# First eight units' K/V and Q products one unit ahead, a new order in the quantising steps, probabilities scaled by GpSimd there

## The chip, the core and the metric

The kernel runs on one core of one Trainium2 chip. The metric is the device time of one launch in microseconds. A core has five engines that run side by side, each through its own queue of instructions in order: TensorE (PE in the rows, with its weight loads as PEld), VectorE (DVE), ScalarE (ACT), GpSimd (POOL) and SyncE (SP, which here only issues transfers). They meet at semaphores: an instruction waits until a counter has reached a value.

## What is computed

Two layers over x, 8 batches of 128 tokens of width 512. A layer is cross attention to a context of the same size (32 query heads and 8 key/value heads of 128, a root-mean-square norm on q and k), added through a tanh gate, and then a feed-forward part, also gated. The first layer's feed-forward multiplies quantised weights and inputs; the second's has 4-bit weights.

```
x = x + tanh(g_xattn[0]) * xattn0(layernorm(x), ctx)
x = x + tanh(g_ffn[0])   * mx_ffn(layernorm(x))
x = x + tanh(g_xattn[1]) * xattn1(layernorm(x), ctx)
x = x + tanh(g_ffn[1])   * int4_linear(layernorm(x))

q = rmsnorm(x @ Wq.T); k = rmsnorm(ctx @ Wk.T); v = ctx @ Wv.T
out = softmax(q k.T / sqrt(128) + mask) v;  return out @ Wo.T
mx_ffn: weights and inputs rounded in blocks of 32 with one power of two
        (weights to 4 bits, inputs to 6)
```

## The kernel before, in words

**Units.** The attention of both layers is cut into 128 units. A unit is one group (one key/value head and its four query heads, 8 groups a layer) for one batch; `n` counts them, and eight in a row share their weights. All products are done in three parts, high x high, low x high and high x low, of values split into a rounded part and the rest, so every operand has a `_hi` and a `_lo`. Rounding to `_hi` is a ScalarE copy, `_lo` a subtraction on VectorE or GpSimd.

**A unit's chain.** TensorE: K and V from the context into bank psKV, Q from the normalised tokens into psQ. ScalarE: squares of K and of the four heads of Q with their sums, V to `v_hi`. GpSimd: `unit_rstd`, the reciprocal root of the five sums (L519, L523). ScalarE scales K to `kn` (L709), VectorE scales Q to `qn` (L1020). TensorE transposes both; `kT` is taken out of the bank by VectorE (L1039), `qT` by ScalarE (L730). TensorE: scores into psSQ. VectorE: scale and mask to `probs` (L1007), then the negative maximum (L902). ScalarE: exponentials and row sums (L639). VectorE: `rinv` (L956), `probs` times `rinv` (L982). TensorE transposes them into psPO; ScalarE takes `pT_hi`, VectorE `pT_lo` (L907). TensorE multiplies with V; ScalarE takes `oT_hi`, VectorE `oT_lo` (L968). TensorE multiplies with the output weights into psY; VectorE adds that to x (L1049).

**Steps.** The chain is spread over four steps: step n does K/V and Q of unit n, the scores of n-1, the transposed probabilities and values of n-2 and the output of n-3. Each engine runs a function `step` of its own, called by `run_steps` for all n; the order of the statements in these functions is the order of the queue, and nothing else sets it. There are five kinds of steps: FIRST (n 0 to 7), QUANT (8 to 47, a loop over groups with eight steps in its body), ZONE (48 to 87, which holds the first feed-forward part), PLAIN (a loop) and LAST.

**FIRST.** It also loads the tokens and the context (two tiles of 128 tokens at a time), normalises a token tile (`moments` on VectorE, `ln_rstd_of` on GpSimd, `normalise`), has TensorE transpose it into psC and splits it (`xT_upper`, `xT_lower`); `t.first` names the tile that a step prepares, the one after its own. The first group's weights are split by `first_upper` and `first_lower` or `first_output_lower`.

**QUANT.** Beside its unit a step splits pieces of the next group's weights, ten a group, at the steps of `SPLIT_STEPS` (0, 1, 2, 1, 2, 1, 2, 1 pieces): `split_upper` on ScalarE (L652), `split_lower` on GpSimd (L485). And in seven of eight steps it quantises a piece of the feed-forward weights (512 columns in step 0, 384 in the others), with VectorE's `piece_scaled` (L830 to L846) and GpSimd's `round_piece` (L532, L534, L537); one step later VectorE turns it (`piece_turned`, L854) and ScalarE copies it away (L696). GpSimd's queue in a step is `split_lower`, `unit_rstd`, `round_piece`.

**ZONE.** Where a feed-forward tile is worked on (`t.active`), GpSimd scales the probabilities (L560) and ScalarE takes `kT`; elsewhere VectorE does both.

## Time and profile before

| | us |
|---|---|
| median of three timed runs | 1380.63 (1380.35 to 1380.7) |
| the profiled execution | 1378.14 |
| its span in the trace | 1376.3 |
| steps 0 to 7 (K/V product of unit 0 at 13.24, of unit 8 at 98.71) | 85.47 |
| steps 8 to 47 | 395.89 |
| step 48 | 10.04 |
| the rest | 871.66 |

Over the span TensorE is busy 98%, VectorE 72%, ScalarE 59%, GpSimd 48%. A share is a mean over stages. What a stage could gain is read from the time between two like instructions of TensorE in neighbouring steps, here the first of the K/V products, against the same time in a stage without waits.

### The profile page before, as it was taken

The numbers are of one execution on the slowest core, as the hardware profiler recorded it, in microseconds if no ns is written. First come the engines' busy times: TensorE is split into PE (matmuls) and PEld (weight loads), VectorE is DVE, ScalarE is ACT, GpSimd is POOL, SyncE is SP. The second block draws the span as 40 slices with busy tenths as digits, with TensorE's granted clock in tenths as the row PEclk, the third lists the DMA queues.
The fourth block names the chain that finished last, engine by engine and source line by source line (L and its number), as shares of the span: only waits on it lengthen the run. The fifth ranks groups of instructions, "written<-read, shape, count | busy, mean of one in ns | idle before, by whom it ended". The sixth has DMA issues, their size and how long they took to land.

```text
span 1376.3 us, 25625 instructions
## 1 busy us (share of the span) xinstructions
PE 1345.1 (98%) x7788; PEld 1130.0 (82%) x7804; DVE 988.4 (72%) x2016; ACT 814.6 (59%) x3255; POOL 660.0 (48%) x686
## 2 busy tenths in 40 slices
PE   4999999999999999999999999999999999999999
PEld 3888888888888888877777788888888888888887
DVE  4678888887888879678887866766555555655656
ACT  4656656565665666555566555655665666655542
POOL 2536656565665657446667533532333324242232
PEclk9999999999999999999999999999999999999999
DMA  8011021212112021010200011201010010100001
GB/s 284 1 47 55 20 64 47 65 48 65 48 32 81 17 66 53 10 36 12 77 32 1 1 31 47 77 31 55 32 46 30 0 47 30 46 30 1 1 9 54
DMA packets 33852, 59.47 MB, mean 43 GB/s; under 512 B 2800, under 2 KB 26224, under 8 KB 29680
## 3 DMA queue, kind: packets, MB, share of 16 engines
q1 hardware_dynamic: 33776, 58.54, 13.0%
q8 instruction: 38, 0.62, 0.2%
q14 instruction: 38, 0.31, 0.1%
HBM read 56.43 MB, written 2.10 MB: 43 GB/s over the span
## 4 chain that ended last, share of the span: by engine, by line
PE 68%; DVE 11%; issue 8%; ACT 7%; POOL 3%; DMA 1%; SPq 0%; ACTq 0%; DVEq 0%; POOLq 0%
PE bank L1164 46%; PE bank L1156 7%; PE bank L1249 5%; PE bank L1298 5%; ACT probs L639 3%; PE bank L1190 3%; DVE pT_lo L907 2%; DVE probs L1007 2%; DVE negmax L902 1%; PE bank L1306 1%; DVE fw_y L838 1%; DVE amax L830 1%; ACT w_hi L652 1%; ACT oT_hi L660 1%; ACT qT L730 1%
## 5 line engine op out<-in xcount | busy, mean ns | idle before, releaser
L485 POOL TENSOR_TENSOR w_lo<-w_raw,w_hi (+1 forms) x150 | 226.8, 1528 | 251.0 <-ACT w_hi L652 251.0
L679 ACT ACTIVATE squares<-bank 128x128 bf16<-128x128 f32 x512 | 134.7, 278 | 217.9 <-PE bank L1164 217.9
L639 ACT ACTIVATE probs<-probs,negmax 128x128 f32<-128x128 f32 x512 | 198.7, 391 | 73.3 <-DVE negmax L902 71.0
L1007 DVE SCALAR_TENSOR_TENSOR probs<-bank,mask_sb 128x512 f32<-128x512 f32 x127 | 87.5, 689 | 204.4 <-PE bank L1249 204.4
L523 POOL TENSOR_TENSOR rstd<-meansq,scalars 128x5 f32<-128x5 f32 x128 | 156.3, 1221 | 10.9 <-POOL meansq L519 1.3
L519 POOL TENSOR_TENSOR meansq<-sumsq,scalars 128x5 f32<-128x5 f32 x128 | 27.4, 214 | 273.6 <-ACT squares L679 273.6
L1164 PE MATMUL bank<-w_hi,oT_hi 128*128 (+1 forms) x512 | 150.9, 416 | 0.0
L1164 PE MATMUL bank<-w_hi,xT_hi 128*128 (+1 forms) x512 | 140.3, 395 | 0.6 <-DVE w_lo L804 0.6
L1164 PE MATMUL bank<-w_lo,oT_hi 128*128 (+1 forms) x512 | 138.2, 391 | 0.0
L1164 PE MATMUL bank<-w_hi,xT_lo 128*128 (+1 forms) x512 | 137.5, 390 | 0.0
L1164 PE MATMUL bank<-w_hi,oT_lo 128*128 (+1 forms) x512 | 137.5, 390 | 0.0
L1164 PE MATMUL bank<-w_lo,xT_hi 128*128 (+1 forms) x512 | 137.2, 390 | 0.0
L1249 PE MATMUL bank<-kT,qT 128*128 128x128 f32 x1024 | 135.2, 275 | 0.0
L1249 PEld LDWEIGHTS bank<-kT,qT 128*128 128x128 f32 x1024 | 124.5, 192 | 0.1
L709 ACT ACTIVATE kn<-bank,rstd 128x128 f32<-128x128 f32 x128 | 47.1, 368 | 115.2 <-POOL rstd L523 115.1
L968 DVE TENSOR_TENSOR oT_lo<-bank,oT_hi 128x512 fp32r<-128x512 f32 x125 | 85.6, 685 | 41.2 <-ACT oT_hi L660 40.4
L1164 PEld LDWEIGHTS bank<-w_lo,oT_hi 128*128 128x128 f32 x512 | 96.2, 188 | 22.5
L1164 PEld LDWEIGHTS bank<-w_lo,xT_hi 128*128 128x128 f32 x512 | 96.1, 188 | 21.4
L1164 PEld LDWEIGHTS bank<-w_hi,oT_lo 128*128 128x128 f32 x512 | 96.1, 188 | 20.6
L1164 PEld LDWEIGHTS bank<-w_hi,xT_lo 128*128 128x128 f32 x512 | 96.1, 188 | 20.0
L679 ACT ACTIVATION_READ_ACCUMULATOR squares<-bank 128x1 f32 x512 | 106.2, 207 | 0.0
L1164 PEld LDWEIGHTS bank<-w_hi,xT_hi 128*128 128x128 f32 x512 | 88.2, 190 | 12.6 <-DVE w_lo L804 0.9
(143 smaller groups left out, 3076.4 us busy)
## 6 DMA issues: line engine op xcount, KB each, us to landing
w_raw<-in_wq SPq DMA_DIRECT2D x16, 1024.0 KB, 4.9
w_raw<-in_wo SPq DMA_DIRECT2D x16, 1024.0 KB, 4.7
fw_raw<-in_ffn_w SPq DMA_DIRECT2D x36, 192.0 KB, 2.3
w_raw<-in_wk SPq DMA_DIRECT2D x16, 256.0 KB, 5.4
w_raw<-in_wv SPq DMA_DIRECT2D x16, 256.0 KB, 5.4
x_sb<-in_x SPq DMA_DIRECT2D x4, 512.0 KB, 9.9
ctx_raw<-in_ctxT SPq DMA_DIRECT2D x4, 512.0 KB, 10.5
fw_raw<-in_ffn_w SPq DMA_DIRECT2D x7, 256.0 KB, 2.6
```

What stands on the lines that cost most here:

```text
L485: last = nc.gpsimd.tensor_tensor(lo, raw, hi.bitcast(FP32), ALU.subtract)
L523: nc.gpsimd.tensor_tensor(rstd[:, :], meansq[:, :], minus_half[:, :], ALU.pow).then_inc(rs_done, 1)
L639: last = nc.scalar.activation(probs[:, h * P:(h + 1) * P], probs[:, h * P:(h + 1) * P], ACT.Exp, bias=negmax[:, h:h + 1], accum_out=rowsum ...
L679: last = nc.scalar.activation(squares[:, h // 2, (b + 1) % 4, h % 2, :], psQ[:, h * P:(h + 1) * P], ACT.Square, scale=SCALE, accum_out=sum ...
L709: nc.scalar.activation(kn[:, :], psKV[:, 0:P], ACT.Copy, scale=rstd[:, REP:REP + 1]).then_inc(kn_done, 1)
L968: nc.vector.tensor_tensor(oT_lo[:, :], psPO[:, :], oT_hi[:, :].bitcast(FP32), ALU.subtract).then_inc(o_lod, 1)
L1007: nc.vector.scalar_tensor_tensor(heads(probs[:, :]), heads(psSQ[:, :]), SCALE, mask_sb[:, :].unsqueeze(1).to_broadcast([P, REP, P]), ALU.m ...
L1156: last = nc.tensor.transpose(dst[:, k * P:(k + 1) * P], src[:, k * P:(k + 1) * P], m)
L1164: last = nc.tensor.matmul(dst, left(a, k), right(b, k), start=(n == 0), stop=(n == len(terms) - 1))
L1190: last = nc.tensor.matmul(ps[:, 0:width], f_xqT[:, k, :], wT[:, col:col + width], start=(k == 0), stop=(k == KT - 1))
L1249: last = nc.tensor.matmul(psSQ[:, h * P:(h + 1) * P], qT[:, h * P:(h + 1) * P], kT[:, :], start=True, stop=True)
L1298: last = nc.tensor.matmul(psPO[:, :], v[:, slot, :], p[:, :], start=(k == 0), stop=(k == 2))
```

## The change

**In FIRST.** Tokens and context are loaded tile by tile, the first of each on ScalarE's queue, in another order (and the context lies in memory by batch). TensorE does K/V and Q of unit n+1 in step n (`first_kv`, `first_q`), with psA and psB as second banks for odd units; Q of unit 7 stands at the end of step 6, and step 7 has neither. Unit 0's Q is done part by part as the pieces are rounded and subtracted. Tile n+2 is prepared in step n. Splits of group 1 come one step later, the first output weights' subtractions go from GpSimd to VectorE, and 37 transposes of the identity into psSQ (`keep_clock`), whose results nobody reads, stand ahead of the first K/V product.

**In QUANT.** TensorE does the scores ahead of the transposed probabilities. ScalarE does the exponentials of a unit at the head of the next step instead of before `kT` and `qT`, the roundings of the weight pieces between V and the squares of Q, and `kT`. VectorE takes the piece's maximum and then `rinv` behind `oT_lo`, and `pT_lo` ahead of `qn`. GpSimd scales the probabilities first, then does the root, then the rounding, and `split_lower` last. Step 48 takes over the exponentials that step 47 leaves. SyncE's `load_group` waits for `kv_ps` too.

Three places show what the queues hold. First, **GpSimd** in a step of QUANT with two split pieces, before:

```order
L485 TENSOR_TENSOR w_lo<-w_raw,w_hi 128x512
...
L485 TENSOR_TENSOR w_lo<-w_raw,w_hi 128x512
...
L519 TENSOR_TENSOR meansq<-sumsq,scalars 128x5
L523 TENSOR_TENSOR rstd<-meansq,scalars 128x5
...
L532 TENSOR_TENSOR fw_y<-fw_y,fw_magic 128x384
L534 TENSOR_TENSOR fw_y<-fw_y,fw_magic 128x384
L537 TENSOR_TENSOR fw_out<-fw_y,blk_pow 128x384
```

and in the change (`w_lo` is a weight piece, `rstd` the unit's roots, `fw_` the quantised piece):

```order
L560 TENSOR_TENSOR probs<-probs,rinv 128x512
...
L519 TENSOR_TENSOR meansq<-sumsq,scalars 128x5
L523 TENSOR_TENSOR rstd<-meansq,scalars 128x5
...
L532 TENSOR_TENSOR fw_y<-fw_y,fw_magic 128x384
L534 TENSOR_TENSOR fw_y<-fw_y,fw_magic 128x384
L537 TENSOR_TENSOR fw_out<-fw_y,blk_pow 128x384
...
L494 TENSOR_TENSOR w_lo<-w_raw,w_hi 128x512
...
L494 TENSOR_TENSOR w_lo<-w_raw,w_hi 128x512
```

The root moved ahead of the two pieces, and the scaling of the probabilities is new at the head.

Second, **VectorE** in such a step, before:

```order
L854 STREAM_TRANSPOSE fw_turned<-fw_out 128x384
L968 TENSOR_TENSOR oT_lo<-bank,oT_hi 128x512
L982 TENSOR_TENSOR probs<-probs,rinv 128x512
...
L987 TENSOR_TENSOR v_lo<-bank,v_hi 128x128
...
L830 TENSOR_REDUCE amax<-fw_raw 128x12
...
L1007 SCALAR_TENSOR_TENSOR probs<-bank,mask_sb 128x512
L1020 TENSOR_TENSOR qn<-bank,rstd 128x512
L907 TENSOR_TENSOR pT_lo<-bank,pT_hi 128x512
L902 TENSOR_REDUCE negmax<-probs 128x4
L1039 TENSOR_SCALAR kT<-bank,scalars 128x128
L1049 SCALAR_TENSOR_TENSOR x_sb<-bank,scalars,x_sb 128x512
```

and in the change:

```order
L877 STREAM_TRANSPOSE fw_turned<-fw_out 128x384
L1003 TENSOR_TENSOR oT_lo<-bank,oT_hi 128x512
...
L843 TENSOR_REDUCE amax<-fw_raw 128x12
L925 RECIPROCAL rinv<-rowsum 128x4
...
L1022 TENSOR_TENSOR v_lo<-bank,v_hi 128x128
...
L1046 SCALAR_TENSOR_TENSOR probs<-bank,mask_sb 128x512
L934 TENSOR_TENSOR pT_lo<-bank,pT_hi 128x512
L942 TENSOR_TENSOR qn<-bank,rstd 128x512
L929 TENSOR_REDUCE negmax<-probs 128x4
L1082 SCALAR_TENSOR_TENSOR x_sb<-bank,scalars,x_sb 128x512
```

`rinv` moved behind the maximum of the piece, `pT_lo` ahead of `qn`, and the scaling and `kT` are gone.

Third, **TensorE** at the start, from unit 0's query product to the transposes of its K and Q, before (bank0 and bank1 are psKV and psQ):

```order
L1164 MATMUL bank1<-w_hi,xT_hi 128x512 x4
L1164 MATMUL bank1<-w_lo,xT_hi 128x512 x4
L1164 MATMUL bank1<-w_hi,xT_lo 128x512 x4
L1156 MATMUL bank7<-ident,f_s 128x128 x4
L1289 MATMUL bank0<-ident,kn 128x128
L1156 MATMUL bank2<-ident,qn 128x128 x4
```

and in the change, from the last third of that product on:

```order
L1210 MATMUL bank1<-w_hi,xT_lo 128x512 x4
L1210 MATMUL bank5<-w_hi,ctx_hi 128x256 x4
L1210 MATMUL bank5<-w_lo,ctx_hi 128x256 x4
L1210 MATMUL bank5<-w_hi,ctx_lo 128x256 x4
L1210 MATMUL bank6<-w_hi,xT_hi 128x512 x4
L1210 MATMUL bank6<-w_lo,xT_hi 128x512 x4
L1210 MATMUL bank6<-w_hi,xT_lo 128x512 x4
L1202 MATMUL bank7<-ident,f_s 128x128 x4
L1291 MATMUL bank0<-ident,kn 128x128
L1202 MATMUL bank2<-ident,qn 128x128 x4
```

Unit 1's K/V and Q, in bank5 and bank6, moved in front of unit 0's transposes.

The diff, cut to its core:

```diff
 SPLIT_STEPS = {1: (0,), 2: (1, 2), 3: (3,), 4: (4, 5), 5: (6,), 6: (7, 8), 7: (9,)}
-SPLIT_STEPS_FIRST = {2: (0, 1), 3: (2, 3), 4: (4, 5), 5: (6, 7), 6: (8, 9)}
+SPLIT_STEPS_FIRST = {3: (0, 1), 4: (2, 3), 5: (4, 5), 6: (6, 7), 7: (8, 9)}
...
-        self.first = s + 1 if kind == FIRST and s + 1 < BATCHES else None
+        self.first = s + 2 if kind == FIRST and s + 2 < BATCHES else None
...
+        def exp_after(kind):
+            return kind == QUANT
...
+        def kv_bank(n, kind):
+            return psA if kind == FIRST and n % 2 else psKV
+        def q_bank(n, kind):
+            return psB if kind == FIRST and n % 2 else psQ
...
+                sp.wait_ge(kv_ps, freed)
                 sp.wait_ge(q_ps, freed)
...
+            load_kv(0, 0, loaded_kv0)
+            sp.dma_start(x_sb[:, 1, :], x[P:2 * P, :]).then_inc(loaded_x[1], 16)
+            load_q(0, 0, loaded_q0)
+            sp.dma_start(ctx_raw[:, 1, :], ctxT[:, 1, :]).then_inc(loaded_ctx[1], 16)
+            sp.dma_start(norm_sb[:, :], norms).then_inc(loaded_small, 16)
+            sp.dma_start(mask_sb[:, :], mask).then_inc(loaded_small, 16)
+            load_tokens(2)
+            load_tokens(3)
+            load_wo(0, 0, loaded_wo0)
+            load_tokens(4)
             sp.dma_start(gates[:, 0:2], g_xattn.partition_broadcast(P)).then_inc(loaded_gates, 16)
             sp.dma_start(gates[:, 2:4], g_ffn.partition_broadcast(P)).then_inc(loaded_gates, 16)
-            load_x(0)
-            load_kv(0, 0, loaded_kv0)
-            load_ctx(0)
-            sp.dma_start(norm_sb[:, :], norms).then_inc(loaded_small, 16)
-            sp.dma_start(mask_sb[:, :], mask).then_inc(loaded_small, 16)
-            load_q(0, 0, loaded_q0)
-            load_x(1)
-            load_ctx(1)
-            load_wo(0, 0, loaded_wo0)
-            for t in (2, 3):
-                load_x(t)
-                load_ctx(t)
+            load_tokens(5)
+            load_tokens(6)
+            load_tokens(7)
             load_q(1, WSLOT, loaded_qkv)
             load_kv(1, WSLOT, loaded_qkv)
             load_wo(1, WSLOT, loaded_wo)
...
+                if t.active or kind == QUANT:
                     pool.wait_ge(rinv_done, n - 1)
                     nc.gpsimd.tensor_tensor(
...
+                if kind in (ZONE, PLAIN):
+                    split_lower(split_pieces(n, b, kind, j))
                 if t.first is not None:
                     ln_rstd_of(t.first)
-                if t.last is not None:
-                    ln_rstd_of(NORM["last", t.last])
-                split_lower(split_pieces(n, b, kind, j))
                 if has(n, 0):
                     unit_rstd(n)
+                if kind == FIRST:
+                    split_lower(split_pieces(n, b, kind, j))
...
                     round_piece(q, b)
+                if kind == QUANT:
+                    split_lower(split_pieces(n, b, kind, j))
...
-            act.wait_ge(loaded_gates, 32)
-            nc.scalar.activation(tanh_gates[:, :], gates[:, :], ACT.Tanh).then_inc(gates_done, 1)
+            act.dma_start(x_sb[:, 0, :], x[0:P, :]).then_inc(loaded_x[0], 16)
+            act.dma_start(ctx_raw[:, 0, :], ctxT[:, 0, :]).then_inc(loaded_ctx[0], 16)
...
+                exp_late = exp_after(kind) or (kind == FIRST and b == BATCHES - 1)
...
-                split_upper(split_pieces(n, b, kind, j))
+                if exp_after(kind) or (kind == ZONE and n == ZONE0):
+                    softmax_exp(n - 1)
+                if kind in (ZONE, PLAIN):
+                    split_upper(split_pieces(n, b, kind, j))
...
+                if kind == QUANT:
+                    split_upper(split_pieces(n, b, kind, j))
...
+                if t.first is not None:
+                    ctx_upper(t.first)
+                if kind == FIRST and b in (1, 2):
+                    if b == 1:
+                        act.wait_ge(loaded_wo0, 16)
+                    first_upper(WO_PIECES[2 * b - 2:2 * b])
+                if kind == FIRST:
+                    scaled_k(n, kind)
...
+                if kind == FIRST:
+                    split_upper(split_pieces(n, b, kind, j))
+                if t.first is not None:
+                    xT_upper(t.first)
...
+                if has(n, 0) and kind != FIRST:
+                    scaled_k(n, kind)
+                if has(n, 1) and t.next is None and t.down is None and not exp_late:
                     softmax_exp(n)
...
+                    if t.active or kind == QUANT:
...
+                if kind == FIRST and b == 0:
+                    act.wait_ge(loaded_gates, 32)
+                    nc.scalar.activation(tanh_gates[:, :], gates[:, :], ACT.Tanh).then_inc(gates_done, 1)
...
+            ctx_upper(0)
             act.wait_ge(loaded_kv0, 32)
-            for k in KV_PIECES:
-                raw, hi, _ = weight_piece(0, k)
-                nc.scalar.activation(hi, raw, ACT.Copy).then_inc(first_hi, 1)
-            ctx_upper(0)
+            first_upper(KV_PIECES)
             xT_upper(0)
             act.wait_ge(loaded_q0, 16)
             first_upper(Q_PIECES)
+            ctx_upper(1)
+            xT_upper(1)
...
-                    dve.wait_ge(exp_done, n - 1)
-                    nc.vector.reciprocal(rinv[:, :], rowsum[:, :]).then_inc(rinv_done, 1)
+                    if kind != QUANT:
+                        row_inverse(n)
...
-                if has(n, 2) and not t.active:
+                if q is not None and b < QSTEPS:
+                    piece_maximum(q, b)
+                if kind == QUANT:
+                    row_inverse(n)
+                if has(n, 2) and not t.active and kind != QUANT:
                     dve.wait_ge(rinv_done, n - 1)
                     nc.vector.tensor_tensor(heads(probs[:, :]), heads(probs[:, :]), each(rinv[:, :], P),
                                             ALU.mult).then_inc(pn_done, 1)
...
+                    if t.first is not None:
+                        ctx_lower(t.first)
...
+                if kind == FIRST:
+                    scaled_q(n, kind, t)
...
-                if has(n, 2) and t.gate is not None:
+                if has(n, 2) and (t.gate is not None or kind == QUANT):
                     probs_lower(n)
...
+                if has(n, 0) and kind != FIRST:
+                    scaled_q(n, kind, t)
+                if has(n, 2) and qn_first(kind, t) and kind != QUANT:
                     probs_lower(n)
                 if has(n, 1) and qn_first(kind, t):
                     maximum(n)
...
+                if has(n, 0) and not t.active and kind != QUANT:
...
+                if t.first is not None:
+                    xT_lower(t.first)
...
+                if kind == FIRST and b + 3 < BATCHES:
+                    dve.wait_ge(loaded_x[b + 3], 16)
+                    moments(b + 3, b + 3)
+                if kind == FIRST and b in (1, 2):
+                    for k in WO_PIECES[2 * b - 2:2 * b]:
+                        first_lower(k, k + 1)
+                if kind == FIRST and b == 1:
+                    dve.wait_ge(gates_done, 1)
+                    nc.vector.tensor_scalar(down_gate[:, :], tanh_gates[:, LAYERS:LAYERS + 1], 1 / FP6_UNIT, None,
+                                            ALU.mult).then_inc(down_gate_done, 1)
...
+            ctx_lower(0)
             for n, k in enumerate(KV_PIECES):
                 first_lower(k, n + 1)
-            ctx_lower(0)
...
+            dve.wait_ge(loaded_x[1], 16)
+            moments(1, 1)
+            dve.wait_ge(xT_ps, 1)
+            normalise(1, 1, f_s[:, :])
             for n, k in enumerate(Q_PIECES):
                 first_lower(k, len(KV_PIECES) + n + 1)
+            ctx_lower(1)
...
+            xT_lower(1)
+            dve.wait_ge(loaded_x[2], 16)
+            moments(2, 2)
             dve.wait_ge(qkw_done, 1)
...
+            def first_kv(u):
...
+                pe.wait_ge(ctx_lo_done, u + 1)
+                if u == 0:
+                    pe.wait_ge(first_lo, len(KV_PIECES))
+                wait(pe, kT_sb, u - 1)
+                three_products(kv_bank(u, FIRST)[:, 0:2 * P], lambda a, k: (ctx_hi, ctx_lo)[a][:, u, k * P:(k + 1) * P],
+                               lambda a, k: (w_hi, w_lo)[a][:, WKV0 + k * 2 * P:WKV0 + (k + 1) * 2 * P]).then_inc(kv_ps, 1)
+            def first_q(u, part=slice(0, 3 * KT)):
+                pe.wait_ge(xT_lod, u + 1)
+                wait(pe, qn_done, u - 1)
+                return three_products(q_bank(u, FIRST)[:, :], lambda a, k: (xT_hi, xT_lo)[a][:, k, xT_tile(u)],
+                                      lambda a, k: (w_hi, w_lo)[a][:, WQ0 + k * REP * P:WQ0 + (k + 1) * REP * P], part)
...
+                if kind == FIRST and b == BATCHES - 2:
+                    first_kv(b + 1)
+                    scores()
+                    probabilities()
+                    output()
+                    transposed()
+                    values()
+                    first_q(b + 1).then_inc(q_ps, 1)
+                    return
+                if kind == FIRST and b == BATCHES - 1:
+                    scores()
+                    probabilities()
+                    output()
+                    transposed()
+                    values()
+                    return
+                if kind == FIRST and b + 1 < BATCHES:
+                    first_kv(b + 1)
+                    first_q(b + 1).then_inc(q_ps, 1)
...
+                if kind == QUANT:
+                    scores()
                 if has(n, 2):
...
+                    probabilities()
+                if has(n, 1) and kind != QUANT:
+                    scores()
...
+            def keep_clock(count):
...
+                for _ in range(count):
+                    nc.tensor.transpose(psSQ[:, 0:P], ident[:, :], ident[:, :])
             pe.wait_ge(consts, 2)
+            keep_clock(21)
             pe.wait_ge(ln_xn, 1)
             transposes(f_s, psC, ident[:, :]).then_inc(xT_ps, 1)
+            keep_clock(16)
+            first_kv(0)
+            for k in range(KT):
+                pe.wait_ge(first_hi, len(KV_PIECES) + k + 1)
+                first_q(0, slice(k, k + 1))
+            pe.wait_ge(ln_xn, 2)
+            pe.wait_ge(xT_lod, 1)
+            transposes(f_s, psC, ident[:, :]).then_inc(xT_ps, 1)
+            for k in range(KT):
+                pe.wait_ge(first_lo, len(KV_PIECES) + k + 1)
+                first_q(0, slice(KT + k, KT + k + 1))
+            first_q(0, slice(2 * KT, 3 * KT)).then_inc(q_ps, 1)
             run_steps(pe, step)
```

## Rows read from the trace of the kernel before

**Rows 1.** Stretches: from:to, length, busy us of each engine, clock, DMA share, GB/s

```profile
98.71:494.60 395.89, 390.56 (x2242) 329.12 (x2241) 330.48 (x716) 241.10 (x1000) 243.29 (x235) 1.00 0.17 52
494.60:504.64 10.04, 9.93 (x58) 8.27 (x56) 8.25 (x20) 6.51 (x30) 4.21 (x5) 1.00 0.15 41
504.64:1376.30 871.66, 866.36 (x5071) 726.93 (x5085) 587.35 (x1173) 509.64 (x2023) 374.42 (x391) 1.00 0.10 31
196.99:207.36 10.37, 10.00 (x58) 8.10 (x57) 9.02 (x20) 6.35 (x26) 7.70 (x8) 1.00 0.16 36
982.94:992.47 9.53, 9.53 (x58) 8.30 (x56) 5.30 (x12) 5.79 (x25) 3.13 (x3) 1.00 0.28 107
```

**Rows 2.** Timeline of a long quantising step: start, length, engine, line, operation

```profile
160.65 2.99 POOL L485 TENSOR_TENSOR w_lo<-w_raw,w_hi  x2 [2.40 <-ACT w_hi L652]
...
162.47 1.20 DVE L835 TENSOR_SCALAR inv_pow<-amax 128x12 uint32<-128x12 uint32 x1
...
163.87 1.56 POOL L523 TENSOR_TENSOR rstd<-meansq,scalars 128x5 f32<-128x5 f32 x1
...
165.31 0.68 DVE L1007 SCALAR_TENSOR_TENSOR probs<-bank,mask_sb 128x512 f32<-128x512 f32 x1
...
165.91 0.68 DVE L1020 TENSOR_TENSOR qn<-bank,rstd 128x512 f32<-128x512 f32 x1
```

**Rows 3.** Waits in 98.7 to 494.6: total us, times, longest

```profile
PEld bank L1156 <- DVE qn L1020: 9.2, 15, 0.6
PEld bank L1164 <- DVE kT L1039: 6.3, 20, 0.3
```

**Rows 4.** Timeline of the first 45 us

```profile
0.74 0.40 SPq L414 DMA_DIRECT2D scalars<-in_g_xattn  x1
...
1.66 0.43 SPq L386 DMA_DIRECT2D x_sb<-in_x  x1
...
7.54 0.69 DVE L786 BATCH_NORM_STATS2 ln_stats<-x_sb 128x6 f32<-128x512 f32 x1 [7.54 <-DMA x_sb<-in_x]
...
11.96 1.23 DVE L809 TENSOR_TENSOR ctx_lo<-ctx_raw,ctx_hi 128x1024 fp32r<-128x1024 f32 x1 [0.70 <-ACT ctx_hi L618]
...
13.56 2.19 ACT L613 ACTIVATE w_hi<-w_raw 128x512 fp32r<-128x512 f32 x4 [1.15 <-DMA w_raw<-in_wq]
...
19.87 0.28 ACT L679 ACTIVATE squares<-bank 128x128 bf16<-128x128 f32 x1 [3.13 <-PE bank L1164]
...
34.50 1.19 PE L1164 MATMUL bank<-w_hi,ctx_hi 128*128 128x256 f32 x4
```

**Rows 5.** Stretches of the first stage, two steps

```profile
34.50:46.65 12.15, 9.91 (x48) 8.72 (x49) 6.76 (x12) 8.42 (x31) 7.64 (x8) 0.78 0.01 2
79.16:89.20 10.04, 10.04 (x62) 8.79 (x62) 8.13 (x15) 6.81 (x27) 5.08 (x6) 1.00 0.01 3
```

**Rows 6.** Timeline of TensorE in a quantising step with one split piece

```profile
168.09 0.75 PE L1164 MATMUL bank<-w_hi,ctx_hi 128*128 x4
...
172.38 0.60 PE L1156 MATMUL bank<-ident,probs 128*128 128x128 f32 x4
172.82 1.06 PE L1249 MATMUL bank<-kT,qT 128*128 128x128 f32 x8
173.63 1.18 PE L1164 MATMUL bank<-w_hi,oT_hi 128*128 x4
...
176.59 0.60 PE L1156 MATMUL bank<-ident,qn 128*128 128x128 f32 x4
176.95 0.48 PE L1298 MATMUL bank<-pT_hi,v_hi 128*128 128x512 f32 x1
```

**Rows 7.** Groups by shape: busy us, mean ns; quantising stage, then GpSimd's scaling in the zone

```profile
L485 POOL TENSOR_TENSOR w_lo<-w_raw,w_hi x39 | 61.8, 1597 | 64.5 <-ACT w_hi L652 64.5
L639 ACT ACTIVATE probs<-probs,negmax 128x128 f32<-128x128 f32 x120 | 46.8, 391 | 52.5 <-DVE negmax L902 52.5
```

```profile
L560 POOL TENSOR_TENSOR probs<-probs,rinv 128x512 f32<-128x512 f32 x15 | 15.6, 1042 | 25.6 <-DVE rinv L956 25.6
```

201 lines of the change are left out of this document (87 added, 114 removed).

## The prediction

> **What bounds the kernel now.** I cut the trace at the starts of TensorE's K/V products, one stretch per step of the schedule, then read one long step of the quantising stage in order of time, the waits of that stage, and the start. TensorE is busy for 390.56 of 395.89 us in one stage and for 866.36 of 871.66 in the rest [rows 1]. So what another engine does costs time only where TensorE waits or runs at its lower clock, and the reader should look for the steps that are longer than TensorE's own work. A step of the second layer, where nothing is waited for, takes 9.53 us [rows 1]; that is what the matmuls and transposes of one unit need. Against this floor two stages are long.
>
> The **quantising stage** (units 8 to 47) takes 395.89 us, 9.90 a step; 40 x 9.53 would be 381.2, so 14.7 us are lost there. They sit mostly in three steps of each eight, which take 10.37 instead of 9.64 [rows 1]: those in which two weight pieces are split. In one of them, in order of time [rows 2], GpSimd subtracts two pieces (2.99 us, to 163.64), and only then makes the unit's reciprocal root (163.87 to 165.43); VectorE's tiny `inv_pow` takes 1.20 while GpSimd works, though it has 12 columns; VectorE's `probs` and `qn` follow, the last done at 166.59, and TensorE waits for `qn` [rows 3]. The other 0.1 of each short step is the wait for `kT` before the next K/V product [rows 3].
>
> The **first stage** (units 0 to 7) lasts until 98.71. Unit 0's query product ends at 19.8 (ScalarE's squares of it start at 19.87, [rows 4]), and from there each unit's chain from its query product to its own transposes lies bare. The step from 34.50 has TensorE busy 9.91 of 12.15 us at a granted clock of 0.78; the last but one takes 10.04 at 1.00 [rows 5].
>
> **First stage, part by part.** *Loads.* The first token tile is half the size and is issued first, on ScalarE's queue, while SyncE starts on the K/V weights. Before, two tiles were issued at 1.66, 0.9 us behind the first small issue, and landed at 7.54 [rows 4]; without the 0.9 and with half the bytes (0.26 MB, shared with the K/V weights, some 0.4) I take 6.2. The query weights landed at 13.56 [rows 4] with 1.6 MB ahead of them; with 1.3 MB ahead and the stream 0.9 us earlier they land at 11.8. *Unit 0.* ScalarE rounds the four query pieces in 2.19 [rows 4], to 14.0. VectorE, which has normalised the second tile meanwhile, subtracts four times (0.68 each, as `qn` in [rows 2]), to 16.9. The last four products end at 17.9: 1.9 us earlier than now. *Units 1 to 7.* From there TensorE has K/V and Q of the next unit to do while the squares, root, scaled K and scaled Q of this one are made. Its work, from one step's rows [rows 6]: K/V and Q 4.2; transposed probabilities 0.44; scores 0.81; output product and transposed K 2.96; transposed Q 0.36; values 0.78. With the next tile's transposes (10.04 less 9.53, so 0.5) step 0 needs 5.2, step 1 6.0, step 2 7.2, steps 3 to 5 10.0 each, step 6 9.5, and step 7, which has no K/V and Q any more, 5.3. Sum 63.2, so 81.1 if nothing waits.
>
> What waits next is **VectorE** in steps 1 and 2. A full step of it is 8.13 busy [rows 5]. In step 2 it has no output residue and no accumulation (two passes, 1.4), but a context residue (half of the 1.23 of two tiles, [rows 4]) and two output weight pieces that GpSimd did before (1.3): 8.6 against TensorE's 7.2. Step 1 has three passes fewer again, 7.1 against 6.0. That is 2.5 us; with 0.4 for unit 0's root, which is done a little after TensorE comes to it, the stage ends at **84.0**, 14.7 us earlier. The filler transposes run while TensorE has nothing else and cost nothing themselves; what they are worth is the clock. Bounds: 81.1 with no wait, and 89, if three K/V products run at the lower clock as that of 34.50 did (its first four matmuls took 1.19, [rows 4], so twelve some 2.7, against 1.5 at the higher) with 1.3 us more in the loads.
>
> **Quantising stage, part by part.** I write a step from the start of its K/V product. *TensorE*: scores now stand at 4.3 and the transposed probabilities at 5.1, output at 5.5, transposed Q at 8.5, values at 8.9, next step 9.6 [rows 6]; without waits 0.1 less each. *ScalarE*: the output copy to 0.8, then the exponentials (four of 0.39, [rows 7]) to 2.5, K's square and V to 3.0, two roundings to 4.2, just before the query product is there at 4.4. So moving the roundings costs nothing, and moving the exponentials takes `rinv` from 1.3 to 2.6. *GpSimd* scales the probabilities from 2.7 in 1.04 (its own time for this in the zone, [rows 7]) to 3.8. TensorE needs them at 5.0: 1.2 to spare. It starts the root at 5.8, to 7.0 alone and to 7.4 at its 1.56 [rows 2]; rounds for 2.9 (its 7.70 of a long step less splits and root, [rows 1, 2]), to 10.2; then subtracts up to two pieces at 1.6 each [rows 7], to 13.4, which is 3.8 of the next step. *VectorE* loses two passes (probabilities and `kT`). Its piece takes 2.84 from `inv_pow` to `probs` [rows 2], with the tiny operation ahead 3.1, and 2.1 without the blocked 1.0; started at 3.4 and let in at 3.8, it gives `probs` 5.9 to 6.6, the residue to 7.2, `qn` at 7.4 to 8.1. TensorE comes to it at 8.4. `kT`, now ScalarE's first work behind its transpose, is ready 0.4 before it is needed, which takes the 0.1 of the short steps away.
>
> What is late next is the steps **behind two split pieces** (steps 3 and 5 of eight) and the one behind the 512-wide piece (step 1): GpSimd starts the scaling at 3.8 only, holds to 4.9, and VectorE's tiny operations, blocked as `inv_pow` was [rows 2], come through at 4.9. Then `probs` ends at 7.5, the residue at 8.1, `qn` at 8.8: TensorE waits 0.4. Three such steps in each of five groups are 6.0, so the stage takes 381.2 + 6.0 = **387.2**, 8.7 less. Bounds: 381.2 (no wait) and 395.2, if all 35 steps that have a piece wait 0.4.
>
> A rule speaks against the GpSimd part. The rows show 1.04 on GpSimd for a pass of the size that takes VectorE 0.68, a ratio of 1.5 [rows 2, 7]. The Trainium skill, GPSIMD Engine Reference, section 4.1 Engine selection, says to use VectorE for elementwise work on a tile, GpSimd being about 2 times slower with two inputs. By that page's ratio the scaling would take an estimated 1.4, end at 5.2 behind two pieces, after TensorE's 5.0, and cost an estimated 3 us more. I go by the row.
>
> **Zone.** From 504.64 on the order is the same, and its 871.66 us stay [rows 1]. Unit 48's step has ScalarE do one more unit of exponentials before its squares, so `rinv` comes at 2.6 and VectorE's scaling, which stands behind its output residue and the piece's maximum there, at 4.9 instead of in time; with its piece behind that, `pT_lo` comes some 1.4 late. The step takes 11.0 instead of 10.04 [rows 1]: +1.0 (bounds 0 and 2). The one more wait in SyncE's weight loads is met together with the old one; behind it stand only loads that are needed a group later.
>
> **Sum**, against the profiled execution: 1378.14 - 14.7 - 8.7 + 1.0 = 1355.7. The three timed runs have a median of 1380.63, 2.5 above the profiled one; I forecast on their level, **1358.2**.
>
> **Rivals.**
> *All waits gone.* First stage to 81.1, quantising 381.2, unit 48 +0.5: 17.6 + 14.7 - 0.5 = 31.8 less, 1348.8. For it: by the steps above each engine but TensorE has time to spare in nearly every step. Against: the blocked 1.20 [rows 2].
> *The two engines block each other in every step.* Scaling and piece start close together in all of them, so the 0.4 comes 35 times: quantising 395.2, and with the rest as forecast 1366.2. By the row one blocked operation costs 1.0; whether all of them are blocked, it doesn't tell. The Trainium skill, SBUF — State Buffer, section Who interferes with whom, says that GpSimd and a VectorE instruction with two inputs in SBUF lock each other out for a whole instruction. It would favour this case, and the 1.20 [rows 2] agrees with it as far as one operation can.
> *The start gains little.* TensorE is at most half busy between 12.5 and 17, and the step from 34.50, behind such a pause, began at half clock. Three cold K/V products (1.2 each) and loads 1 us later: stage to 88.6, 1362.8.
> *Slower.* Each piece of VectorE meets the scaling (1.04) and the root as well, so that `qn` comes at 8.1 + 1.0 + 1.3 = 10.4 and 35 steps wait 2.0: quantising 451, sum 1422. It is slower than before from a mean step of 10.24 on (the 13.7 us of the other parts spread over 40 steps of 9.90). Against: GpSimd has 7.70 + 1.04 = 8.7 us of work in the fullest step [rows 1, 7], under 9.53, and the order puts the root ahead of the long subtractions.
>
> **How the numbers follow.** Forecast 0.50, all waits gone 0.20, blocking in every step 0.16, weak start 0.09, slower 0.05. The range reaches from the second case to a little above the third and fourth, 1349 to 1370; about 2 in 10 are left out, the slow case and the tails. A measurement of this kernel can tell about 0.2%, 2.8 us, from no change. Faster by more than that 0.93, within it 0.02, slower 0.05.
>
> **What would show it.** First stage: the K/V product of unit 8 at 84 instead of 98.71, the first squares at 18, and a granted clock of 1.00 from unit 1 on. Quantising: steps of 9.53 to 9.55 after one split piece, 9.9 after two; the waits for `kT` gone, that for `qn` left at some 6 us; `inv_pow` still far over 0.2 in the mean. A scaling that ends after 5.0 of its step, or a TensorE that waits for `probs`, would make the forecast wrong; so would a first K/V product later than 12.

## The result and the profile after

The changed kernel takes 1346.98 us (median of 4 runs, 1346.24 to 1347.88), the kernel before beside it 1380.49 (4 runs). The ratio is 0.9762 (95% interval 0.9745 to 0.9779): 33.5 us faster. The forecast was 1358.2, with a range down to 1349. The direction held, and the gain was half as large again as foretold. What came true, within 2 us, is the rival in which all waits go (1348.8).

The profiled execution took 1346.36 us, its span is 1344.4. Cut into the same stretches as before [rows 1] (from:to, length, busy us of PE, PEld, DVE, ACT, POOL, granted clock, DMA share, GB/s):

```profile
0.00:81.13 81.13, 77.63 (x459) 66.09 (x460) 58.66 (x119) 55.27 (x201) 33.80 (x52) 1.00 0.39 139
81.13:462.57 381.44, 381.44 (x2241) 333.65 (x2242) 299.32 (x636) 265.78 (x1045) 263.97 (x276) 1.00 0.17 53
462.57:472.81 10.24, 10.16 (x57) 8.19 (x56) 7.71 (x19) 6.65 (x32) 4.41 (x5) 1.00 0.16 44
472.81:1344.40 871.59, 867.33 (x5087) 726.96 (x5085) 587.39 (x1173) 509.22 (x2023) 373.93 (x391) 1.00 0.09 31
128.90:138.43 9.53, 9.53 (x57) 8.34 (x56) 7.98 (x17) 6.55 (x27) 7.70 (x9) 1.00 0.09 24
```

Unit 8's K/V product starts at 81.13 (98.71 before, 84.0 forecast). The quantising stage takes 381.44 (395.89 before, 387.2 forecast), and TensorE is busy in all of it. Step 48 takes 10.24 (10.04; 11.0), the rest 871.59 (871.66). The last row is a step behind one with two split pieces, the kind for which 9.9 was forecast: it takes 9.53, as all but the first do (9.64). The profile's page follows the chain of work that ended last. TensorE has 96% of that chain now, and had 68% before:

```profile
PE 96%; DVE 1%; POOL 1%; issue 1%; DMA 0%; ACT 0%; SPq 0%; POOLq 0%; DVEq 0%; ACTq 0%
```

The start, in order of time (start, length, engine, line, operation); it answers to [rows 4]:

```profile
0.73 0.39 ACTq L610 DMA_DIRECT2D x_sb<-in_x  x1
...
3.59 0.69 DVE L804 BATCH_NORM_STATS2 ln_stats<-x_sb 128x6 f32<-128x512 f32 x1 [3.59 <-DMA x_sb<-in_x]
...
6.49 1.16 ACT L617 ACTIVATE w_hi<-w_raw 128x512 fp32r<-128x512 f32 x2 [0.66 <-DMA w_raw<-in_wv]
...
8.60 0.71 PE L1210 MATMUL bank<-w_hi,ctx_hi 128*128 128x256 f32 x4
...
9.66 2.19 ACT L617 ACTIVATE w_hi<-w_raw 128x512 fp32r<-128x512 f32 x4 [1.53 <-DMA w_raw<-in_wq]
...
15.36 0.28 ACT L694 ACTIVATE squares<-bank 128x128 bf16<-128x128 f32 x1 [1.46 <-PE bank L1210]
```

The token tile is used at 3.59 instead of 7.54 (forecast 6.2), the query weights are there at 9.66 instead of 13.56 (forecast 11.8), and the first squares start at 15.36 instead of 19.87.

The quantising step at 128.90, behind two split pieces; it answers to [rows 2]:

```profile
129.36 2.55 POOL L494 TENSOR_TENSOR w_lo<-w_raw,w_hi  x2
...
131.86 1.05 POOL L560 TENSOR_TENSOR probs<-probs,rinv 128x512 f32<-128x512 f32 x1
131.89 1.04 DVE L855 TENSOR_SCALAR amax<-amax 128x12 f32<-128x12 f32 x1
132.97 0.17 DVE L858 TENSOR_SCALAR inv_pow<-amax 128x12 uint32<-128x12 uint32 x1
...
133.98 0.60 PE L1202 MATMUL bank<-ident,probs 128*128 128x128 f32 x4
...
135.00 1.17 POOL L523 TENSOR_TENSOR rstd<-meansq,scalars 128x5 f32<-128x5 f32 x1
...
136.21 0.69 DVE L942 TENSOR_TENSOR qn<-bank,rstd 128x512 f32<-128x512 f32 x1
...
137.30 0.60 PE L1202 MATMUL bank<-ident,qn 128*128 128x128 f32 x4
```

Two things stand here. VectorE's first tiny operation beside the scaling takes 1.04 us, about as long as GpSimd scales, as forecast. But the two pieces take 2.55, not 3.2: GpSimd is free at 131.86, 2.96 after the step's start and not 3.8. So `qn` is done at 136.90, 8.0 after the start, 0.4 before TensorE comes to it. In the list of waits of this stage no wait of TensorE for another engine is left; the ones of [rows 3] are gone, both.

### The profile page after: what moved, and what is told of

It is laid out like the page before. It is cut to its first block, busy times and chain, and to the rows that moved or that the text cites. A ratio compares the mean times of both kernels' runs of the same rounds, so it can differ in the third digit from the quotient of the medians.

```text
span 1344.4 us, 25718 instructions
## 1 busy us (share of the span) xinstructions
PE 1336.6 (99%) x7841; PEld 1134.9 (84%) x7841; DVE 953.1 (71%) x1944; ACT 836.9 (62%) x3299; POOL 676.1 (50%) x722
## 4 chain that ended last, share of the span: by engine, by line
PE 96%; DVE 1%; POOL 1%; issue 1%; DMA 0%; ACT 0%; SPq 0%; POOLq 0%; DVEq 0%; ACTq 0%
PE bank L1210 66%; PE bank L1202 9%; PE bank L1274 8%; PE bank L1301 7%; PE bank L1236 3%; PE bank L1395 1%; PE bank L1291 1%; PE bank L1407 1%; DMA w_raw<-in_wv 0%; DVE w_lo L823 0%; PE bank L1382 0%; POOL probs L560 0%; POOL rstd L523 0%; DVE probs L1046 0%; POOL f_s L513 0%
## 5 line engine op out<-in xcount | busy, mean ns | idle before, releaser
L494 POOL TENSOR_TENSOR w_lo<-w_raw,w_hi (+1 forms) x150 | 210.7, 1420 | 174.9 <-ACT w_hi L661 174.9
L523 POOL TENSOR_TENSOR rstd<-meansq,scalars 128x5 f32<-128x5 f32 x128 | 153.6, 1200 | 10.7 <-POOL meansq L519 1.1
L1274 PEld LDWEIGHTS bank<-kT,qT 128*128 128x128 f32 x1024 | 127.5, 191 | 3.3
```

The costliest lines, as they stand in the source:

```text
L494: last = nc.gpsimd.tensor_tensor(lo, raw, hi.bitcast(FP32), ALU.subtract)
L523: nc.gpsimd.tensor_tensor(rstd[:, :], meansq[:, :], minus_half[:, :], ALU.pow).then_inc(rs_done, 1)
L1274: last = nc.tensor.matmul(psSQ[:, h * P:(h + 1) * P], qT[:, h * P:(h + 1) * P], kT[:, :], start=True, stop=True)
```

## The experiments

All are measured beside the kernel before. "After" means 1346.98 us with a quantising stage of 381.44. Times are medians of 4 runs (5 for order_to_55); starts and lengths of steps come from one trace each. Unit 0's part of the start varies from trace to trace: in the ten traces with the same loads, filler and order up to unit 0's query product, its K/V product starts between 8.52 and 9.82, and the query weights are used between 9.44 and 10.91. After has 8.60 and 9.66.

### The two halves apart

**start_only**: the new first stage, the old order in the quantising steps.

```
         def exp_after(kind):
-            return kind == QUANT
+            return False
...
-                if kind in (ZONE, PLAIN):
+                if kind in (QUANT, ZONE, PLAIN):
                     split_lower(split_pieces(n, b, kind, j))
...
-                if has(n, 2) and not t.active and kind != QUANT:
+                if has(n, 2) and not t.active:
```

> The first stage of the changed kernel with the quantising steps of the kernel before (VectorE scales the probabilities, the split pieces stand ahead of the root, the exponentials at their old place, kT on VectorE, scores after the transposes of the probabilities). Theory (the two halves are independent and add): unit 8's K/V product at 81.1 as in the changed kernel, units 8 to 47 take 395.9 as before, step 48 10.04, and the time is 1380.5 - 17.6 = 1362.9 us. Rival (the order in the quantising steps helps the start as well, or an early start leaves the first quantising step late): unit 8 later than 82, time over 1364.5.

1361.46 us. Unit 8 at 81.06, units 8 to 47 in 396.13.

**order_only**: the kernel before with the new quantising steps.

```
-                if t.active:
+                if t.active or kind == QUANT:
                     pool.wait_ge(rinv_done, n - 1)
...
                     round_piece(q, b)
+                if kind == QUANT:
+                    split_lower(split_pieces(n, b, kind, j))
...
+                if kind == QUANT or (kind == ZONE and n == ZONE0):
+                    softmax_exp(n - 1)
```

> The kernel before with the quantising steps of the changed one, and the first stage as before (its last exponentials move to step 8, as the new order needs). Theory (the halves add): unit 8 at 98.7, units 8 to 47 in 381.4, step 48 about 10.2, time 1380.5 - 14.3 = 1366.2 us; a split piece on GpSimd takes 1.3 us here instead of the 1.6 before, since it no longer lies beside VectorE's quantiser. Rival (the steps are short only after the new start): over 1370.

1366.18 us. Unit 8 came at 101.39, and from there to unit 48 it took 381.33. Against the runs of before beside them (1380.18) the halves give 18.7 and 14.0 us, 32.7 together, where both at once give 33.5: they add, within 1 us. In both the mean of a split piece came out as the order has it, 1.60 us with the old and 1.30 with the new.

That unit 8 came 2.7 us later than in the profile of before, in code that is the same up to there but for one group of exponentials, I put down to the clock. Most of it lies in unit 0's query product. Its first four matmuls, before and then in order_only, with the same start within 0.1 us:

```profile
16.78 1.21 PE L1164 MATMUL bank<-w_hi,xT_hi 128*128 128x512 f32 x4 [0.61 <-DVE w_lo L804]
```

```profile
16.84 2.08 PE L1183 MATMUL bank<-w_hi,xT_hi 128*128 128x512 f32 x4 [0.62 <-DVE w_lo L812]
```

The operands are there at the same time in both and TensorE waits for none within it; the clock is given as 1.00 for both, so that the durations alone speak for it here. The stretches of the first stage in order_only show a lower one in that column too:

```profile
13.29:26.19 12.90, 9.55 (x33) 7.62 (x34) 6.36 (x15) 4.72 (x17) 2.12 (x4) 0.93 1.06 389
26.19:37.34 11.15, 9.08 (x42) 7.61 (x42) 6.62 (x10) 6.55 (x24) 4.65 (x6) 0.78 0.49 169
37.34:49.05 11.71, 9.79 (x48) 8.13 (x49) 6.76 (x12) 7.92 (x31) 7.64 (x8) 0.82 0.01 2
49.05:60.30 11.25, 11.25 (x62) 9.73 (x61) 8.14 (x15) 7.41 (x27) 5.10 (x6) 0.88 0.00 1
```

With the old start TensorE pauses for 1.9 to 3.4 us in each of the first three steps, and the granted clock is under 1.00 in four. In the profiled run of before the clock was back at 0.96 in the fourth:

```profile
46.65:57.90 11.25, 11.21 (x63) 9.24 (x62) 8.38 (x15) 7.35 (x28) 5.08 (x6) 0.96 0.00 1
```

In the changed kernel that column gives 1.00 throughout the stage. Nearly all runs of before lie within 0.3 us of 1378.0 or of 1380.4, and few between; a start that in one run loses 1.9 us more in one product would make such levels. It isn't shown that it does: the mean clocks of the runs don't tell the levels apart (1377.99 and 1380.3 both have 0.998).

### What in the quantising steps carries the gain

**vector_scales**: VectorE scales the probabilities in them, as before; all else is changed.

```
-                if t.active or kind == QUANT:
+                if t.active:
                     pool.wait_ge(rinv_done, n - 1)
...
-                if has(n, 2) and not t.active and kind != QUANT:
+                if has(n, 2) and not t.active:
                     dve.wait_ge(rinv_done, n - 1)
```

> The changed kernel, but VectorE scales the probabilities in the quantising steps, in the place where GpSimd's scaling blocked it. Theory A (the GpSimd scaling gives VectorE little, because VectorE's next instruction took 0.73 us on average instead of 0.17 while GpSimd scaled): VectorE's chain ends 0.3 us later, the product's slack of 0.4 us before the transposes of qn takes it, and the time stays at 1346.5 to 1348.5 us. Theory B (GpSimd's scaling carries a good part of the 14.4 us that the quantising steps gained): 1352 us or more, with TensorE waiting for qn in every long step.

1347.56 us, the stage 381.43:

```profile
81.49:462.92 381.43, 381.43 (x2240) 333.61 (x2241) 306.38 (x676) 265.74 (x1045) 223.03 (x236) 1.00 0.17 53
```

The scaling on GpSimd is worth nothing that can be measured. VectorE is busy 306.38 us instead of 299.32, 7 more, although 40 passes went back to it: in the changed kernel it pays most of them as blocked time.

**splits_before_root**: GpSimd splits ahead of the root again, but behind the scaling.

```
-                if kind in (ZONE, PLAIN):
+                if kind in (QUANT, ZONE, PLAIN):
                     split_lower(split_pieces(n, b, kind, j))
...
-                if kind == QUANT:
-                    split_lower(split_pieces(n, b, kind, j))
```

> The changed kernel, but GpSimd splits the weight pieces ahead of the unit's root in the quantising steps, behind the scaling. Theory (where the splits stand is what the steps hang on): in a step with two pieces scaling ends at 4.0, two pieces beside VectorE's quantiser at 1.6 each end at 7.2, root at 8.8, qn at 9.5 and its transposes 1.1 us later than the TensorE work allows, x 15 such steps = 16.5 us: 1363.5 us; steps with one piece stay at 9.53; a piece takes 1.6 us on average. Rival (only the amount of GpSimd work counts): 1347 to 1349 and pieces of 1.3 us.

1369.01 us, 22.0 more than after. A step with two pieces takes 10.65 (10.6 by the theory). Of the four with a single piece in each eight, three take 9.71, 9.71 and 10.18 and not 9.53; the last one, in which nothing is quantised, stays at 9.53:

```profile
132.26:141.98 9.72, 9.72 (x57) 8.29 (x56) 8.65 (x18) 6.56 (x27) 6.45 (x8) 1.00 0.09 24
141.98:152.63 10.65, 9.95 (x57) 8.29 (x56) 9.55 (x18) 7.07 (x28) 8.11 (x9) 1.00 0.08 25
```

That the place of the pieces decides held, but the 10.6 came true by luck. The theory went over the root: two pieces of 1.6, then the root, then `qn`. In the step from 141.98 the root is over at 7.98, 0.8 earlier than laid out, and `qn` starts only at 8.73. What is late is VectorE, held up beside each piece:

```profile
145.60 2.52 POOL L494 TENSOR_TENSOR w_lo<-w_raw,w_hi  x2
145.70 1.20 DVE L856 TENSOR_SCALAR inv_pow<-amax 128x12 uint32<-128x12 uint32 x1
...
147.01 1.52 DVE L859 SCALAR_TENSOR_TENSOR fw_y<-fw_raw,inv_pow 128x384 f32<-128x384 f32 x1
...
148.67 1.29 POOL L523 TENSOR_TENSOR rstd<-meansq,scalars 128x5 f32<-128x5 f32 x1
...
150.71 0.68 DVE L940 TENSOR_TENSOR qn<-bank,rstd 128x512 f32<-128x512 f32 x1
```

`inv_pow` takes 0.17 and `fw_y` 0.56 where GpSimd is idle; here the two lose 2.0 us. The root alone would have let `qn` end at 8.7, for which TensorE would have waited some 0.3 (an estimate from these rows). In [rows 2] it was the same: the root was over at 165.43, and `qn` began at 165.91, behind VectorE's own chain.

A piece took 1.28, not 1.6, though the pieces now lay beside VectorE's quantiser, which I had taken for the cause. This is the quantising stage's group of pieces in start_only, and then in splits_before_root (count, busy us, mean ns):

```profile
L494 POOL TENSOR_TENSOR w_lo<-w_raw,w_hi (+1 forms) x51 | 80.8, 1596 | 83.9 <-ACT w_hi L659 83.9
```

```profile
L494 POOL TENSOR_TENSOR w_lo<-w_raw,w_hi (+1 forms) x51 | 64.7, 1281 | 0.0
```

What differs is seen in the timeline of start_only. A single piece takes 1.75 there, two take 2.99, so the second costs 1.24 and only the first is long:

```profile
133.80 1.75 POOL L494 TENSOR_TENSOR w_lo<-w_raw,w_hi  x1 [2.67 <-ACT w_hi L659]
...
143.21 0.68 DVE L1008 TENSOR_TENSOR probs<-probs,rinv 128x512 f32<-128x512 f32 x1
143.28 2.99 POOL L494 TENSOR_TENSOR w_lo<-w_raw,w_hi  x2 [2.40 <-ACT w_hi L659]
```

The first piece starts 0.07 into VectorE's scaling, a pass with two inputs in SBUF, and takes 0.45 longer than a piece alone. The "1.6 each" of [rows 7] is 1.28 a piece and one wait of 0.45 behind that pass: in each eight steps seven of the ten pieces are first ones, and 0.7 x 0.45 and 1.28 make 1.60. In splits_last_only, which follows, VectorE still scales and the pieces are moved: their mean is 1.30.

**splits_last_only**: start_only, and of the new order nothing but GpSimd's split pieces at the step's end.

```
-                if kind in (QUANT, ZONE, PLAIN):
+                if kind in (ZONE, PLAIN):
                     split_lower(split_pieces(n, b, kind, j))
...
                     round_piece(q, b)
+                if kind == QUANT:
+                    split_lower(split_pieces(n, b, kind, j))
```

> The new first stage with the old quantising steps, and of the new order only that GpSimd splits the weight pieces at the end of a step (after round_piece) instead of ahead of the root. Theory (the place of the split pieces is what the 14.4 us of the quantising steps hang on): the 10.34 us steps with two pieces become 9.63 like the others, 15 x 0.7 = 10.5 us, and steps 8 to 47 take 385 to 386: 1361.5 - 10.5 = 1351 us; what is left to 1347 are the waits of 0.1 us a step for kT. Rival (the move works only together with the early exponentials and scores, because a piece at the head of the next step blocks VectorE's scaling there): over 1356.

1348.59 us. The stage takes 383.79 instead of 396.13: moving these few lines gives 12.3 of its 14.7 us. VectorE's tiny operations take 0.17 each in it. What is left, 2.4 us, goes with the wait of TensorE's weight loads for `kT`, in 25 steps (they run ahead of the matmuls, so a wait of 0.3 makes a step only some 0.1 longer):

```profile
PEld bank L1204 <- DVE kT L1064: 6.4, 25, 0.3
```

**kT_on_vector**: after, with `kT` scaled by VectorE.

```
-                    if t.active or kind == QUANT:
+                    if t.active:
                         layer = layer_of(n, 0, kind)
                         act.wait_ge(kt_ps, n + 1)
...
-                if has(n, 0) and not t.active and kind != QUANT:
+                if has(n, 0) and not t.active:
                     dve.wait_ge(kt_ps, n + 1)
```

> The changed kernel, but VectorE scales kT again in the quantising steps. Theory (with pT_lo now ahead of qn only the maxima stand between qn and kT, which ends 0.5 us before the next unit's K/V product needs the bank): no step longer than 9.54, time 1346.5 to 1347.5 us. Rival (the move to ScalarE is what took the waits for kT away): 0.1 us again in each of 40 steps, 1351 us.

1346.95 us, no step of the stage over 9.54. So ScalarE's taking `kT` isn't needed either; together with splits_last_only it says that the last 2.4 us come from the rest of the new order. In it `pT_lo` stands ahead of `qn`, so that only the maxima are between `qn` and `kT`. Which of its parts is enough was not tried.

**scaling_twice**: after, with GpSimd scaling twice in each quantising step. The probabilities are divided by the row sums twice, so the values differ; the operations and their sizes are otherwise the same.

```
                     pool.wait_ge(rinv_done, n - 1)
+                    if kind == QUANT:
+                        nc.gpsimd.tensor_tensor(
+                            probs[:, :].rearrange("p (h c) -> p h c", h=REP), probs[:, :].rearrange("p (h c) -> p h c", h=REP),
+                            rinv[:, :].unsqueeze(2).to_broadcast([P, REP, P]), ALU.mult).then_inc(copied, 1)
+                        pool.wait_ge(copied, n - (BATCHES - 1))
```

> The changed kernel with GpSimd scaling the probabilities twice in each quantising step (so they are divided by the row sums twice, and the output isn't the reference's): 1.04 us more of the same work in the same place. It measures the slack behind the scaling. Theory: VectorE's chain (piece, masked scores, pT_lo, qn) moves back by the 1.0 us that its next instruction is blocked once more; the slack of 0.4 us before the transposes of qn takes part, 0.6 us stay in about 35 steps: 1347 + 20 = 1367 us, with waits for qn. Rival (there is slack all through the step, as the short steps suggest): 1347 to 1349 us.

1353.63 us, 6.7 more where 20 were expected, and the stage takes 388.16. Of each eight steps three stay at 9.53, the three behind two split pieces take 9.75, the one behind the 512-wide piece 9.78, and the one that has this piece itself 10.00. TensorE's waits in the stage (total, times, longest):

```profile
PEld bank L1208 <- DVE qn L948: 4.1, 10, 0.6
PEld bank L1208 <- POOL probs L566: 3.4, 15, 0.5
```

So the slack behind the scaling is 1.0 us or more in 15 steps, 0.8 in 20 and 0.6 in 5. The kinds of wait differ. Behind two pieces TensorE waits for the probabilities, the second scaling being over 5.2 after the step's start; the 10 waits for `qn` are in the other two kinds. The step from 111.80 (behind two pieces):

```profile
114.79 0.16 DVE L861 TENSOR_SCALAR amax<-amax 128x12 f32<-128x12 f32 x1
...
115.95 1.04 POOL L566 TENSOR_TENSOR probs<-probs,rinv 128x512 f32<-128x512 f32 x1
...
116.01 1.40 DVE L867 SCALAR_TENSOR_TENSOR fw_y<-fw_raw,inv_pow 128x384 f32<-128x384 f32 x1
...
117.04 0.42 PEld L1208 LDWEIGHTS bank<-ident,probs 128*128 128x128 f32 x4 [0.20 <-POOL probs L566]
```

I had expected VectorE's whole chain to slip by 1.04. Its first tiny operation slipped in ahead of the scaling (0.16), and the second scaling held `fw_y` up by 0.84, so the masked scores start 0.7 later than in the step shown of after. `qn` starts at 7.79 against 7.31, only 0.5 later: the other 0.2 are the time for which it had to wait for the root in after (over at 136.17).

### The first stage

**no_unit_ahead**: the products of units 1 to 7 at the head of their own step.

```
-                if kind == FIRST and b == BATCHES - 2:
+                if kind == FIRST and b:
+                    first_kv(b)
+                    first_q(b).then_inc(q_ps, 1)
+                if False:
...
-                if kind == FIRST and b == BATCHES - 1:
+                if False:
...
-                if kind == FIRST and b + 1 < BATCHES:
+                if False:
```

> The changed kernel, but in units 1 to 7 the K/V and Q products stand at the head of their own step again, in the order of before; loads, filler transposes and the tile preparation are as changed. Theory (being one unit ahead carries most of the first stage's gain beyond the 4.5 us at the very start): TensorE waits again for the chain squares, root, qn in each step, unit 8 at about 93, time 1359 us. Rival (the earlier loads, the full clock and the tile by tile preparation carry it): unit 8 before 84, time under 1350.

1363.95 us, unit 8 at 98.75: all 17.6 us gone. But TensorE waits here for something that this edit alone brings in, the next normalised tile:

```profile
PEld bank L1202 <- DVE f_s L810: 9.4, 5, 2.2
```

`f_s` stands behind the context's residue on VectorE, that behind ScalarE's rounding, and that behind the squares of this unit's query product, which is harmless only as long as the product came a step earlier.

**no_unit_ahead_ctx_early**: the same, with ScalarE rounding the context ahead of the squares.

```
                     nc.scalar.activation(v_hi[:, b % 4, :], kv_bank(n, kind)[:, P:2 * P], ACT.Copy).then_inc(v_hid, 1)
+                if t.first is not None:
+                    ctx_upper(t.first)
...
                     last.then_inc(sq_done, 1)
-                if t.first is not None:
-                    ctx_upper(t.first)
```

> As no_unit_ahead (products of units 1 to 7 at the head of their own step), with one thing mended: ScalarE rounds the next tile's context ahead of the unit's squares instead of behind them, so that VectorE's normalised tile no longer hangs on this unit's query product. Theory (being one unit ahead itself is worth most of the first stage, since in units 0 to 2 TensorE has nothing to do while squares, root and scaled query are made, some 3 us each, and falls to its lower clock there): unit 8's K/V product at 91 to 95, time 1357 to 1360 us. Rival (most of the 17 us that no_unit_ahead lost was the wait for the normalised tile, 8.5 to 9.4 us in its list): unit 8 before 90, time under 1356 us.

1359.21 us, unit 8 at 91.48, and the whole quantising stage at 9.53 a step. So being one unit ahead is worth 10.3 us of the 17.6, clock included. In the first three steps (11.86, 9.48 and 10.73) TensorE stands idle for 3.4, 2.5 and 2.1 us, and the granted clock is 0.90 to 0.94 up to the fourth; of the first:

```profile
9.02:20.88 11.86, 8.49 (x37) 5.47 (x38) 8.94 (x20) 6.25 (x20) 3.40 (x6) 0.90 0.94 341
```

There TensorE has too little else to do while squares, root and scaled query are made. Steps one unit ahead can't be laid beside these one by one, since theirs hold the next unit's products. From unit 4 on the steps take 9.97, as they do one unit ahead.

**gates_first**: the two small broadcast loads at the head of SyncE's queue.

```
+            sp.dma_start(gates[:, 0:2], g_xattn.partition_broadcast(P)).then_inc(loaded_gates, 16)
+            sp.dma_start(gates[:, 2:4], g_ffn.partition_broadcast(P)).then_inc(loaded_gates, 16)
             load_kv(0, 0, loaded_kv0)
```

> The changed kernel with the two small broadcast loads of the gates at the head of SyncE's queue, as before; x0 and ctx0 stay on ScalarE's queue, nobody waits for the gates before step 0. Theory (the broadcast loads were what made all data start late before, where the transfers moved nothing until 4.2 us): the K/V weights land 2 us or more later than at 6.5 us, unit 0's K/V product starts at 10.5 or later, and the time is 1349 us. Rival (they cost their two issues of 0.45 us and no more): product at 9.5, 1347.9 us.

1348.45 us. Their issues take 0.9 us, but unit 0's K/V product starts at 10.58, 2.0 us later than in after and 0.8 later than in the latest of the ten traces with the same start; the query weights are used at 11.63, unit 8 starts at 83.12. Even the tile on the other queue came later, at 4.67 where the other traces with it on that queue have 3.26 to 3.66:

```profile
4.67 0.69 DVE L804 BATCH_NORM_STATS2 ln_stats<-x_sb 128x6 f32<-128x512 f32 x1 [4.67 <-DMA x_sb<-in_x]
```

**first_tile_on_sync**: x0 ahead of, and ctx0 behind, the K/V weights on SyncE's queue.

```
-            act.dma_start(x_sb[:, 0, :], x[0:P, :]).then_inc(loaded_x[0], 16)
-            act.dma_start(ctx_raw[:, 0, :], ctxT[:, 0, :]).then_inc(loaded_ctx[0], 16)
+            sp.dma_start(x_sb[:, 0, :], x[0:P, :]).then_inc(loaded_x[0], 16)
             load_kv(0, 0, loaded_kv0)
+            sp.dma_start(ctx_raw[:, 0, :], ctxT[:, 0, :]).then_inc(loaded_ctx[0], 16)
```

> The changed kernel with x0 (first) and ctx0 (behind the K/V weights) on SyncE's queue, none on ScalarE's. Theory (what matters is the size of x0, 256 KB instead of 512, and that nothing is ahead of it): statistics at 3.6 again, ctx0 is issued at 2.5 instead of 1.15 and the Q weights 0.9 us later, so unit 0's K/V product comes at 9.0 to 9.5 and the time is about 1347.9 us. Rival (the second queue is what brought x0 at 3.6 instead of the 6.2 forecast): statistics at 5.5 or later, time 1349 us or more.

1347.90 us, unit 0's product at 9.55, which is inside the spread of the unchanged start. The four runs (1347.72 to 1348.01) overlap with those of after, so a cost of 0.9 us isn't certain. The tile is used at 3.40, so the second queue isn't what brings it early:

```profile
3.40 0.69 DVE L804 BATCH_NORM_STATS2 ln_stats<-x_sb 128x6 f32<-128x512 f32 x1 [3.40 <-DMA x_sb<-in_x]
```

**no_filler**: without the 21 and 16 transposes that compute nothing used.

```
-            keep_clock(21)
...
-            keep_clock(16)
```

> The changed kernel without the 21 and 16 filler transposes ahead of the first products (they compute nothing that is used). Theory (they only keep TensorE's clock up for unit 0's products): unit 0's products at the lower clock take up to twice their 1.4 and 2.8 us, the first squares come 1 to 3 us later, and the time is 1348 to 1350 us. Rival (the clock rises in the real work as fast): the same within 0.5 us.

1347.63 us. From the start of unit 0's K/V product to the first squares it takes 7.7 us, where the ten traces with the filler have 5.9 to 6.8. That product, without the filler:

```profile
8.96 1.19 PE L1210 MATMUL bank<-w_hi,ctx_hi 128*128 128x256 f32 x4 [2.06 <-DVE w_lo L823]
9.96 1.05 PE L1210 MATMUL bank<-w_lo,ctx_hi 128*128 128x256 f32 x4
```

With it:

```profile
8.60 0.71 PE L1210 MATMUL bank<-w_hi,ctx_hi 128*128 128x256 f32 x4
9.15 0.64 PE L1210 MATMUL bank<-w_lo,ctx_hi 128*128 128x256 f32 x4
```

From its first matmul to its last the product takes 1.7 us with the filler and 2.9 without. What of this 1.2 reaches the time can't be told: the medians are 0.65 us apart and the runs overlap. The granted clock of both stretches is given as 1.00, so here the durations tell more than that column.

### A version that might have been better

**order_to_55**: the new order kept through steps 48 to 55.

```
-        def exp_after(kind):
+        def early(n, kind):
-            return kind == QUANT
+            return kind == QUANT or (kind == ZONE and n < FFN0)
...
-                if has(n, 2) and not t.active and kind != QUANT:
+                if has(n, 2) and not t.active and not early(n, kind):
```

> The changed kernel with the new order of the quantising steps kept through steps 48 to 55, which quantise the last group and split two weight pieces in each of five steps. Theory (the same 0.2 us a step and the 0.7 us of step 48 can be had there too, GpSimd's 8.1 us of work a step fit into 9.53): steps 48 to 54 at 9.53, 1.9 us less, 1345.1 us. Rival (two pieces at the end of every step push the scaling of the next one so far back that TensorE waits for the probabilities): steps of 9.7 us or more, 1347 us or worse.

1350.20 us, 3.2 slower than after (five runs, 1349.76 to 1351.72). Steps 48 to 50 take 9.53 instead of 10.24 and 9.74, as expected. Then step 51 takes 12.54, step 52 11.18 and step 55 10.36. TensorE stops ahead of unit 52's K/V product:

```profile
501.15 2.49 POOL L495 TENSOR_TENSOR w_lo<-w_raw,w_hi 128x512 fp32r<-128x512 f32 x2
```

```profile
503.70 1.00 PE L1211 MATMUL bank<-w_hi,ctx_hi 128*128 128x256 f32 x4 [2.84 <-POOL w_lo L495]
504.49 1.05 PE L1211 MATMUL bank<-w_lo,ctx_hi 128*128 128x256 f32 x4
```

Unit 52 is the first of the next weight group, and its last K/V pieces are split in step 51. At that step's end they are too late. The matmuls after the pause run at 1.05 for four instead of 0.64, and the granted clock of step 52 is 0.85:

```profile
503.70:514.88 11.18, 11.18 (x56) 9.83 (x57) 5.49 (x13) 4.95 (x18) 4.63 (x6) 0.85 0.06 19
```

The rival's time came true (1347 or worse), but not by its way, the steps 48 to 50 staying at 9.53; neither case named the group's boundary. With the order changed back at step 51 some 0.4 us would be left to gain (0.7 + 0.2 + 0.2 in steps 48 to 50, less the 0.7 that the change back costs in step 48 now); that is an estimate from the steps' lengths, less than can be measured here, and no run has it. No kernel here beats the changed one.

## Why the prediction was wrong, point by point

The sum was 1378.14 - 14.7 - 8.7 + 1.0 = 1355.7, put at 1358.2 on the level of the timed runs. The profiled execution is 1346.36, 9.3 less; the timed median is 11.2 less.

- **The bound** (TensorE, 9.53 a step, 14.7 us lost in the quantising stage): right. The stage went to 381.44, with a floor of 381.2.
- **Loads**: the term was mis-sized. I took 6.2 for the first tile and 11.8 for the query weights; they were used at 3.59 and 9.66. I corrected the time before for what was ahead and for half the bytes, and priced the two small broadcast loads at their issues (0.9 us). gates_first shows them at 2.0 us for the K/V product and the query weights (used at 11.63), less sure by the 1.3 us by which the same start varies, and a tile on another queue delayed by 1.1. What follows in unit 0 took 5.5 us from the landing to the next unit's K/V product (15.16), where 6.1 were laid out; that product was expected at 17.9. 2.7 us.
- **Units 1 to 7**: 66.1 us forecast, 65.97 measured (15.16 to 81.13). The steps are 5.43, 7.16, 8.06, 10.02, 9.94, 9.98, and 15.38 for the last two, where 5.2, 6.0, 7.2, three of 10.0 and 14.8 were the work and 1.1 and 1.4 more were expected in the second and third. TensorE counts as busy for 64.81 of it, so a good half of what I had put down to VectorE was work that I had laid out too small. The sum is right by luck: two errors cancel.
- **Unit 48**: 11.0 forecast, 10.24 measured, 0.8 us.
- **Quantising stage**: this is the step of the prediction that failed. "GpSimd starts the scaling at 3.8 only" rests on two pieces at 1.6 each. They take 1.28, which is 0.65 of the 0.84 by which the scaling starts earlier, at 2.96; GpSimd also comes to them 0.2 earlier, at 10.0 of its step instead of 10.2. The blocked operation of VectorE came as forecast (1.04), but 0.9 us earlier (over at 4.0 instead of 4.9), and the 0.4 of wait turned into 0.4 of slack: 15 waits, 5.8 us. The mean of 1597 ns in [rows 7] was the price in the old order, and 0.45 of each step's first piece was a wait behind VectorE's scaling, which the change moves elsewhere. I used a duration measured under a contention that the change itself removes. How far the rest of the mechanism was sound is shown in part. scaling_twice has waits in the kinds of step that I named, behind two pieces and behind the 512-wide one (and in that one itself, which I didn't name). But behind two pieces they are 0.2 us and for the probabilities, not for `qn`. No run has a single scaling that starts at 3.8; from the rows of after, in which `qn` ends 4.0 after the blocked operation with 0.2 of that spent on the root, I put the wait that it would have brought at 0.3 (an estimate).
- **What was read beside the rows**: GpSimd's first piece took 0.45 longer when it began 0.07 into VectorE's scaling, which has two inputs in SBUF and takes 0.68. The rule for two inputs of the Trainium skill (SBUF — State Buffer, section Who interferes with whom) agrees with that. It was no support for the 1.20 of `inv_pow`, as I had it: that operation, like the `amax` that took 1.04 beside GpSimd's scaling and 0.16 ahead of it, has one input. The rival that the rule was to favour didn't come, since the 0.9 us lost lay in slack. The factor of 2 of the Trainium skill (GPSIMD Engine Reference, section 4.1 Engine selection) isn't what the scaling shows: 1.05 against 0.68 is 1.5. By scaling_twice the scaling would have had to be some 0.6 us longer to cost anything in the first place.
- **The level**: 2.5 us of the forecast were the distance of the timed runs of before from their profiled one. After, that distance is 0.6. That the other 1.9 come from the old start and its clock fits what order_only shows of the old start, and is itself not shown.

The terms add up: 2.9 in the first stage (2.7 for loads and unit 0, 0.1 for units 1 to 7), 5.8 in the quantising stage and 0.8 in step 48 are 9.5, against 9.3 in the profiled execution (0.1 of the rest lies outside the trace's span). With 1.9 for the level they make the 11.2.

Where the 33.5 us come from, by the medians of the runs: 12.9 from the place of GpSimd's split pieces (start_only to splits_last_only), 1.6 from the rest of the quantising order, 12.2 from the products one unit ahead (by the profiles 10.3; that kernel's runs spread from 1356.8 to 1360.7), 1.5 from the late broadcast loads, perhaps 0.9 from x0 and ctx0 on the other queue and 0.6 from the filler, neither of them clear of the spread. Each was measured by taking it out alone, so the sum is only a guide. Some 4 us are left that I didn't separate: the tile by tile preparation, the residues moved to VectorE, and what these parts do for one another. The scaling on GpSimd and `kT` on ScalarE are worth nothing that these runs can tell.

## What to carry to other kernels

If two engines hold each other up, a duration of one is a price only in the order in which it was measured: look at what lay beside each instance (here the first piece of each step was long, the second not) before multiplying the mean. Where a kernel is bound by one engine, look for the chain that makes that engine's latest input, and for what holds that chain up. In the quantising stage, moving work that nobody waits for out of the way of that chain gave 12.3 of 14.7 us, and dividing the work among engines gave nothing. A forecast that comes true can still have the wrong reason (10.6 in splits_before_root), so look in the trace for what was late. Where work is put off to a step's end, look for the place where its result is first needed (the first unit of a weight group) and not only at the mean step.

## What the runs showed of the hardware that I had not expected

- Two broadcast loads of 1 KB at the head of a queue delayed the following data by 2.0 us at their user against after (0.8 against the latest of ten like starts), with 0.9 us of issues, and a 256 KB load on another queue by 1.1 (at 4.67, where eleven other traces have 3.26 to 3.66).
- A GpSimd pass of 128x512 with two inputs took 1.28 us, and 1.75 when it began beside a VectorE pass with two inputs in SBUF. Of two in a row only the first was longer. The other way round, VectorE's operations with one input (128x12) took 1.04 to 1.20 beside such a pass instead of 0.17, and with two inputs (128x384) 1.52 instead of 0.56.
- After the pause of 2.8 us in order_to_55 four matmuls of 256 columns took 1.05 us instead of 0.64. The granted clock is 0.85 in that step, and 0.999 in the mean of the run, which hides it. In no_filler the same 1.05 stands in a stretch for which the clock is given as 1.00, so a clock given as 1.00 this early in a run doesn't show that TensorE ran at full speed.
